# A recurrence of 512 steps: root as exp(0.5 ln), chunk-boundary work spread over its iterations, state rescaled in the fourth step

## The reference, cut to what matters

```
r, g = sigmoid(x Wr'), sigmoid(x Wg');  k, v, a, kk = x Wk', x Wv', x Wa', x Wb'
w = clip(exp(-base_decay) * exp(-exp(x Wt')), 0.01, 0.99)
def step(state, ...):                 # per batch and head: state is 16 x 16
    sa = einsum('bhij,bhj->bhi', state, -kk_t)
    state = w_t[..., None] * state + sa[..., None] * (kk_t * a_t)[:, :, None, :] \
            + k_t[..., None] * v_t[:, :, None, :]
    norm = sqrt(mean(state * state, axis=-1, keepdims=True))
    state = state / (norm + 1e-5)
    o_t = sum(state * r_t[..., None], axis=-1)
out = g * outs @ Wo'; out = x_g + out / (sqrt(mean(out*out)) + 1e-6) * ln_weight
```

## Time and profile before

| what | us |
|---|---|
| median of three runs | 3172.87 |
| profiled execution, own time | 3171.76 |
| its span, first to last instruction | 3170.0 |
| attention and first feed-forward layer, to the last feature tile | 0 to about 973 |
| features and projections ahead of the recurrence | 975 to 1073 |
| the 512 steps with their boundaries | 1081 to 2883 |
| last outputs | 2883 to about 2950 |
| second feed-forward layer | to 3170 |

### The profile page before, as it was taken

The page is one execution under the profiler, slowest core; times in us unless marked ns, Lnnn a source line. Parts: engine busy times, 40 slices in busy tenths (PEclk is TensorE's granted clock), DMA queues, the critical chain, the costliest instruction groups (busy, mean ns, idle before and its releaser), DMA issues. The chain is left out here.

```text
span 3170.0 us, 45730 instructions
## 1 busy us (share of the span) xinstructions
PE 2122.5 (67%) x12323; PEld 1690.7 (53%) x12323; DVE 2395.2 (76%) x6141; ACT 1430.4 (45%) x3369; POOL 723.7 (23%) x1068
## 2 busy tenths in 40 slices
PE   6778888776776766566566676665675664344677
PEld 3545555453445666466566566565565664333344
DVE  5555556556773399999999999999999899995566
ACT  3343334344664444444444444444444444332566
POOL 0000000000000233433434434334334334332000
PEclk7665555666888677666777666777666665665788
DMA  4000000000000000000000000000000000000000
GB/s 142 10 9 6 3 9 9 9 6 0 0 0 0 0 0 0 0 0 0 1 0 0 1 0 0 1 0 0 1 0 0 1 0 0 0 0 0 9 25 20
DMA packets 14135, 20.96 MB, mean 7 GB/s; under 512 B 1281, under 2 KB 12033, under 8 KB 13825
## 3 DMA queue, kind: packets, MB, share of 16 engines
q1 hardware_dynamic: 14080, 20.36, 2.1%
HBM read 12.27 MB, written 4.19 MB: 5 GB/s over the span
## 5 line engine op out<-in xcount | busy, mean ns | idle before, releaser
L619 PE MATMUL bank<-U,ident 128*128 128x128 f32 x2048 | 466.9, 400 | 289.2 <-DVE U L1195 289.2
L619 PEld LDWEIGHTS bank<-U,ident 128*128 128x128 f32 x2048 | 435.4, 274 | 318.0 <-issue 252.9
L598 PE MATMUL bank<-stack,tm 128*128 128x64 f32 x1792 | 342.2, 378 | 223.9 <-ACT tm L695 223.9
L598 PEld LDWEIGHTS bank<-stack,tm 128*128 128x128 f32 x1792 | 331.1, 288 | 243.9 <-issue 243.9
L867 ACT ACTIVATE xs<-U 128x256 f32<-128x256 f32 x512 | 213.5, 417 | 528.4 <-DVE U L1195 527.2
L1150 DVE TENSOR_REDUCE pn<-xs 128x32 f32<-128x512 f32 x512 | 351.2, 686 | 75.5 <-ACT xs L867 32.1
L1252 POOL TENSOR_TENSOR wu<-U,stg 128x256 f32<-128x256 f32 x384 | 238.3, 621 | 737.1 <-DVE U L1195 737.1
L1217 POOL TENSOR_TENSOR kv<-stg 128x256 f32<-128x256 f32 x520 | 321.9, 619 | 17.4 <-ACT stg L801 16.0
L837 ACT ACTIVATE small<-pn 128x16 f32<-128x16 f32 x512 | 110.7, 216 | 415.7 <-DVE pn L1150 415.7
L667 ACT ACTIVATE prob<-bank,nmax 128x128 f32<-128x128 f32 x512 | 145.6, 367 | 244.8 <-DVE nmax L975 244.0
L1209 POOL TENSOR_TENSOR R<-R 128x1024 f32<-128x1024 f32 x8 | 18.9, 2368 | 1035.6 <-ACT R L705 1035.6
(11 more groups left out here) (186 smaller groups left out, 4109.1 us busy)
## 6 DMA issues: line engine op xcount, KB each, us to landing
out_x<-x SPq DMA_DIRECT2D x8, 512.0 KB, 2.9
x<-in_x SPq DMA_DIRECT2D x1, 3584.0 KB, 16.9
Vs<-V SPq DMA_DIRECT2D x8, 272.0 KB, 3.4
lane<-in_lanes SPq DMA_DIRECT2D x8, 256.0 KB, 3.1
wcat<-in_wcat SPq DMA_DIRECT2D x1, 1792.0 KB, 13.7
Vs<-V SPq DMA_DIRECT2D x8, 204.0 KB, 2.7
wraw<-in_w_up SPq DMA_DIRECT2D x1, 1024.0 KB, 18.9
wraw<-in_w_down SPq DMA_DIRECT2D x1, 1024.0 KB, 10.9
```

The source lines that it names most:

```text
L598: last = pe.matmul(bank[3 + g][:, e * CH:(e + 1) * CH], tm[:, g * (PB // 2) + e, :, :].rearrange("p a c -> p (a c)"), stack[:, :], start=T ...
L619: last = pe.matmul(rsum.rearrange("p (t i) -> p t i", i=HD), ident[:, :], steps[:, :, :, j], start=(j == 0), stop=(j == HD - 1))
```

## The change

1. The root becomes two functions, `Ln` and then `Exp` with scale 0.5 (`root`). All functions that ACT uses in the recurrence are of one set, which is loaded once ahead of it. The output's norm does the same.
2. The boundary between chunks is taken out. Its work is done for 8 steps at a time, in slots of ACT and POOL within each iteration: retention (exp, add decay, exp, clip), gates as ln(1 + exp(-x)), logarithms of sigma from a history `hist`, one exponential of the negated sum as the factor (`fac`) of the row sums. DVE keeps a ring of 4 sigmas in PSUM (`sring`) and copies it to `hist` in steps 1 and 5. The products w and kk a are staged by POOL. `R` becomes a ring of 128 rows.
3. Rescaling moves to steps 3 and 7: the difference is multiplied by `lam` = 1/sigma, and kv0 is added without sigma. The small operations `wl`, `pl` and `sl` go. `kkz` holds kk and kka of 4 steps in PSUM.
4. Sigma stands between the p-kka product and the difference; the product of sigma with kv0 waits for the difference too.
5. The slots of ACT are ordered anew: evacuation of the outputs and one part of the output's norm move behind the `Square` of their step.

```
+            def root(t1):
+                act.wait_ge(S["pn"], t1)
+                act.activation(lnr, pn[:, 1, :], ACT.Ln, scale=1.0 / HD).then_inc(S["ln"], 1)
+                act.wait_ge(S["ln"], t1)
+                act.activation(rt, lnr, ACT.Exp, scale=0.5).then_inc(S["rt"], 1)
...
                                 if j == 7:
                                     evacuate_pairs(n, m, 1)
-                                    evacuate_outputs(n, m)
                                 act.wait_ge(S["u"], t0 + (j + 1))
                                 act.activation(xs[:, 1, :], U[:, half, j, :], ACT.Square).then_inc(S["sq"], 1)
+                                if j == 0:
...
+                                    stage_kk(1 - half, row_next)
+                                if j == 1:
+                                    log_norms(it, 1 - half, it * 2 + 1)
+                                if j == 2:
+                                    factors(it, 1 - half)
+                                if j == 3:
+                                    retention(0, it + 1, row_next)
+                                if j == 4:
+                                    gates(1, it, row_it)
+                                if j == 5:
+                                    retention(1, it + 1, row_next)
                                     output_rms(n, m, 1)
                                 if j == 7:
+                                    evacuate_outputs(n, m)
...
+                            dve.wait_ge(S["pn"], t1)
+                            dve.tensor_tensor(ij(zz), col(pn[:, 0, :]), row(kkz[:, jj, 1, :]), ALU.mult).then_inc(S["z"], 1)
...
+                            if jj == RENORM - 1:
+                                dve.wait_ge(S["z"], t1)
+                                if g == 0:
+                                    kk_rows(half, 1)
...
                             dve.wait_ge(S["rt"], t1)
...
+                                dve.scalar_tensor_tensor(sring[:, jj - 1, :], sring[:, (jj + 2) % RENORM, :], LN_EPS, rt,
+                                                         ALU.mult, ALU.add).then_inc(S["sg"], 1)
                             dve.wait_ge(S["z"], t1)
                             dve.wait_ge(S["wu"], t1)
                             dve.tensor_tensor(zz, wu[:, :], zz, ALU.subtract).then_inc(S["d"], 1)
...
+                            dve.wait_ge(S["sg"], t1)
                             dve.wait_ge(S["d"], t1)
+                            if jj == RENORM - 1:
+
+                                dve.reciprocal(lam, sring[:, jj - 1, :]).then_inc(S["lam"], 1)
...
+                                dve.wait_ge(S["lam"], it * 2 + (g + 1))
+                                dve.tensor_tensor(ij(zz), ij(zz), col(lam), ALU.mult).then_inc(S["z2"], 1)
+                                dve.wait_ge(S["z2"], it * 2 + (g + 1))
+                                dve.wait_ge(S["k0"], t1)
+                                new = kv0[:, j % 2, :]
+                            else:
+                                dve.wait_ge(S["k0"], t1)
+                                dve.tensor_tensor(ij(kv[:, :]), col(sring[:, (jj + 3) % RENORM, :]), ij(kv0[:, j % 2, :]),
+                                                  ALU.mult).then_inc(S["k"], 1)
...
+                            dve.tensor_tensor(U[:, half, j, :], zz, new, ALU.add).then_inc(S["u"], 1)
```

More of the change, by code:

```diff
@@ L51 @@
 QKK, QW, QKKA, QK, QV, QR, QG = range(7)
+TKK, TKKA, TW, TK, TV = range(5)
+E_MAX = 1e18
 PAIRS = 7 * HD
@@ L679, in _ @@
             act.wait_ge(ld_w, NLW)
-            act.activation(decay[:, :], decay[:, :], ACT.Exp, scale=-1.0).then_inc(C["fn"], 1)
             act.wait_ge(ini, NINI)
@@ new lines, in stage_kv, with retention @@
+            def stage_kv(half, row):
+                act.activation(stg[:, half, :, TK:TV + 1, :].rearrange("p t q i -> p t (q i)"),
+                               R[:, bass.ds(row, STEPS), QK * HD:(QV + 1) * HD], ACT.Copy).then_inc(G["kv"], 1)
+            def retention(part, k, row):
+                if part == 0:
+                    act.wait_ge(G["e2"], k)
+                    act.activation(wtmp[:, :, :], R[:, bass.ds(row, STEPS), QW * HD:(QW + 1) * HD], ACT.Exp).then_inc(G["e1"], 1)
+                else:
+                    act.wait_ge(G["wd"], k + 1)
+                    act.activation(wtmp[:, :, :], wtmp[:, :, :], ACT.Exp, scale=-1.0).then_inc(G["e2"], 1)
@@ new lines, in gates, with log_norms @@
+            def gates(part, k, row):
+                if part == 0:
+                    act.wait_ge(G["g2"], k)
+                    act.activation(ge[:, :, :], R[:, bass.ds(row, STEPS), QR * HD:], ACT.Exp, scale=-1.0).then_inc(G["g1"], 1)
+                else:
+                    act.wait_ge(G["gm"], k + 1)
+                    act.wait_ge(G["f1"], k)
+                    act.activation(gl[:, :, :], ge[:, :, :], ACT.Ln, bias=1.0).then_inc(G["g2"], 1)
+            def log_norms(k, half, last):
+                act.wait_ge(S["h"], last)
+                act.wait_ge(G["f2"], k)
+                act.activation(ls[:, :, :], hist[:, half, :, :], ACT.Ln).then_inc(G["ls"], 1)
@@ L777, in _ @@
                 running = 0 <= n < NCH
[L778 to L793, removed]
[L794 to L805 removed]
+                if n == 0:
+                    act.wait_ge(C["rc"], NB * 2)
+                    stage_kk(0, 0)
+                    stage_kv(0, 0)
+                    retention(0, 0, 0)
+                    retention(1, 0, 0)
+                if n == NCH:
+                    root(L + 1)
+                    log_norms(L // STEPS, 1, L // RENORM + 1)
+                    row_sums(L // STEPS)
+                    factors(L // STEPS, 1)
                 if yt is not None and yt >= 1:
@@ new lines, in outputs @@
+            def outputs(k, row):
+                pool.wait_ge(G["fc"], k + 1)
+                pool.wait_ge(S["rse"], k + 1)
+                pool.tensor_tensor(ov[:, bass.ds(row, STEPS), :], rs[:, :, :], fac[:, :, :], ALU.mult).then_inc(O["ov"], 1)
+            pool.wait_ge(ini, NINI)
+            a_times_kk(0, 0, 0)
+            retention_add(0)
+            pool.wait_ge(G["e2"], 1)
+            retention_clip(0, 0)
+            pool.wait_ge(G["kv"], 1)
+            outer_product(0, 0)
+            for n in range(NCH):
+                if n >= 2:
+                    pool.wait_ge(O["os"], (n - 1) * NB)
```

344 lines of the change are left out of this document (163 added, 181 removed).

## The result

The changed kernel takes 3182.08 us (median of 10 runs, 3180.13 to 3185.89), the kernel before 3171.09 beside it (10 runs, 3163.26 to 3177.96): ratio 1.0039, 95% interval 1.0030 to 1.0049. That is 0.4% slower, little but clear of the noise. The profiled execution took 3183.05, its span is 3181.3.

The account below looks back on a forecast made before the run. DVE's closed loop of seven dependent operations was taken as the bound. 64 x 27.40 + 52 + 17 = 1822.6 against 1802.2 us, +20.4, less 4.8 at the start, gave 3188 us; 8-in-10 range 3154 to 3222.

Parts of the forecast that it names:

- Boundaries, "127 us gained, 147 lost": Recurrence: removing seven chunk boundaries gains 127 us; longer steps and the stall lose 147.
- Sigma, 0.50 behind the product: Plain step on DVE: with a two-operation root, sigma starts 0.50 us behind the p-kka product instead of 0.34.
- Product with kv0, 0.53 behind the difference: Plain step on DVE: sigma times kv0 also waits for the difference, starting 0.53 us behind it instead of 0.33.
- Plain step 3.27: DVE loop in steps 0, 1, 2, 4, 5, 6: start to start 3.27 us against 3.04.
- 64 x 27.40: Recurrence: 64 iterations of eight steps without stalls, 27.40 us each.
- Fourth step 3.82, step 7 4.00: Steps 3 and 7, with kk copy and rescaling: 3.82 us in place of 3.2; 4.00 in step 7.
- Stall 1.07, 51 us: Square of step 2 waits 1.07 us for late PE in chunks 1 to 6: 48 times, 51 us.
- Work beside it, 17 us: Convolution's addition and the output's four operations cost 17 us in the recurrence; other ACT and POOL work fits its gaps.
- Start -4.8, end 0: Outside the recurrence: the start gets about 4.8 us shorter, the end together 0.
- Rival 1: PE is not late, row sums still start at S+0.2: 40 us less, 3148 us, faster; chance 0.18.
- Rival 2: POOL's new small operations hold DVE up in the recurrence: 29 us at worst, 3217 us; chance 0.12.
- Rival 3: Logarithm and exponential reload ACT's function table at each use: 1311 us more, 4480 in all; chance 0.01.

Follow-up runs that it names:

- b_root_two: Kernel before with its square roots split into Ln and Exp and its starting state adapted: 3203.96 us, ratio 1.0107.
- root_three: Changed kernel with a third ACT operation, a copy of 16 columns, added to the root: 3236.05 us, ratio 1.0209.
- kv_free: Changed kernel with sigma times kv0, and the reciprocal in steps 3 and 7, no longer waiting for the difference: 3115.97 us, ratio 0.9817.
- wait_order: Changed kernel with the wait for the difference coded last of three before the product with kv0: 3192.02 us, ratio 1.0060.
- wait_first: Changed kernel with the wait for the difference coded first of three before the product with kv0: 3165.14 us, ratio 0.9976.
- few_regs: kk_two with semaphore counts chosen so that the step's own two numbers serve all loop waits, needing fewer register instructions: 3154.38 us, ratio 0.9949.
- evac_ahead: Changed kernel with the evacuation of the outputs moved back ahead of the Square of step 7: 3141.96 us, ratio 0.9895.
- b_evac_behind: Kernel before with the evacuation of the outputs moved behind the Square of step 7: 3209.28 us, ratio 1.0122.
- pool_twice: Changed kernel with one more POOL multiplication of 128 columns, result unused, in steps 1, 2 and 5: 3183.07 us, ratio 1.0049.
- kk_two: Changed kernel with kk rows copied two steps at a time before the reductions of steps 0, 2, 4, 6: 3171.42 us, ratio 0.9997.

## Why the prediction was right

The forecast was 3188 us and slower, the result is 3182 and slower: 15 us above before were forecast, 11.0 measured. In its own steps:

- **Boundaries, "127 us gained, 147 lost".** 123.5 gained (120.9 and 2.6) and 140.7 lost. Right.
- **Sigma, 0.50 behind the product.** 0.50; b_root_two gives 0.16 for a second operation, the other 0.09 of it being hidden, and root_three 0.25 for a third, of which nothing is hidden. But against before this is a loss in steps 1, 2, 5 and 6 only: steps 0 and 4 of before were no plain steps (3.25 to 3.48 and 3.32, with rescaling), and became shorter. The text called them plain and set 3.27 "against 3.04"; the sum was made against the whole 1802.2, so this did no harm there, but b_root_two was misjudged by it.
- **Product with kv0, 0.53 behind the difference.** 0.51, and kv_free shows that the wait is the cause: without it 0.33. The reason given, a wait in a separate instruction, holds (wait_order, wait_first).
- **Plain step 3.27.** 3.25 in steps 1, 2, 5 and 6, and 3.19 in steps 0 and 4. What the prediction had wrong there is "from the start to the p-kka product nothing changes: 1.24". The start of steps 0 and 4 is held 0.09 by the register instruction ("the next start has one register instruction"), ACT's `Square` is not, so it leads by 0.11 and the reduction comes 0.45 and not 0.52 behind the start. 12 us of the 64 x 27.40 (measured 64 x 27.21, from step lengths without stalls) are mostly this. few_regs loses just this lead.
- **Fourth step 3.82, step 7 4.00.** 3.815 and mostly 3.98 to 4.11, but 4.29 to 4.36 in the output chunks 3, 5 and 7.
- **Stall 1.07, 51 us.** Right place, too small: 1.2 in chunks 1, 3 and 5, mostly 1.3 in 2, 4 and 6, 61.6 us with chunk 0, where it is 0.31 and not 0.08. In chunks 1 to 6, 0.02 to 0.15 of the excess is that the row sums start at S+1.05 and S+1.19 and not at S+1.03, the rest that steps 0 to 2 are together 0.11 shorter and so arrive earlier.
- **Work beside it, 17 us.** 1819.3 less 64 x 27.21 less 61.6: 16.
- **Start -4.8, end 0.** From the last evacuation of R to the first start it was 8.57 (1072.26 to 1080.83) and is 2.31, so 6.3 were gained where 6.1 was forecast. The rest of that term can't be told in a start that varies by 16 us between runs. From the last S to the end it is 287.8 against 287.0.
- **Rival 1 (PE not late)** is out by evac_ahead and b_evac_behind; it did name what turns the sign. **Rival 2** is out by pool_twice. **Rival 3** wasn't run; the trace after has no table load in the recurrence. What the prediction took from the Trainium skill (SBUF — State Buffer, "SBUF: two separate sides") agrees with pool_twice as far as it goes: every DVE operation of the loop there reads at most one operand from SBUF, and none grew. The row against it, a product with two SBUF inputs that took 0.42 beside a POOL operation, stays unexplained.

The sum came to +20.4 and is +17.1 because two misses offset each other: 12 us too much for the steps, 10 too little for the stall. So the mechanism is right and the closeness of the total is in part luck. The profiled execution was forecast at 3187.4 and took 3183.05: 3.3 us of this are the recurrence, 1.9 the start (6.7 less, 4.8 forecast), which varies by more than that, and at the end 0.9 comes back.

## What to carry to other kernels

When an evacuation or another release is moved on an engine with slack, ask which engine waits for it and whether what hangs on that engine ends just in time: here one call, placed behind the next operation of its engine instead of ahead of it, delayed PE by 0.84 to 1.17 us in each of 48 iterations, cost 44 us and turned a gain into a loss. In a loop of dependent operations count waits like operations: put the wait that blocks first, leave out those that only repeat the order, and choose semaphore counts so that few numbers serve all of them. Work shortened ahead of a fixed arrival of another engine is waited away, so move the consumer before tuning those steps.

## What the runs showed of the hardware

- With the same three waits ahead of it, a DVE operation started 0.45, 0.51 or 0.55 us after the start of its 0.42 us predecessor, by whether the wait that blocks is coded first, second or last (wait_first, the changed kernel, wait_order).
- A register instruction between the end of one wait and the next operation costs 0.09: next start 0.55 behind the sum instead of 0.46, sigma 0.59 behind the product instead of 0.50 (kk_two against the changed kernel and few_regs).
- `Ln` and `Exp` of 128x16 take 0.22 each like the copy in root_three, and a chain of them on ACT costs 0.25 a link.
- POOL operations with two SBUF operands (0.46 for 128 columns, 0.62 for 256) left DVE operations that read at most one operand from SBUF at the same length, 686 ns for the reduction in both traces.
- A DVE operation that reads PSUM started 0.33 behind a 0.42 us one that was still writing another part of the same bank (kv_free).
